# Output stage of a decoder layer: sixteen steps of two token tiles in place of eight steps of four

## The reference, cut to what matters

```python
z = out.reshape(B, H, S, dh).transpose(0, 2, 1, 3).reshape(B, S, L)   # (4, 1024, 256)
z = z @ Wo
z = _l2_normalize(z)
z = z @ Wff
z = _l2_normalize(z)
z = jax.nn.gelu(z, approximate=False)
...
x = _layernorm(x + z, axis=-1)      # mean, variance, (x - m) / sqrt(v + 1e-5)
```

## Time and profile before

| what | us |
|---|---|
| median of 3 runs | 1892.95 (1890.54 to 1895.87) |
| the profiled execution, its own time | 1888.5 |
| its span, first to last instruction | 1886.7 |
| first squares of the output stage, from the span's start | 1810.87 |
| mean granted TensorE clock, share of full speed | 0.988 |

### The profile page before, as it was taken

The page is one execution under the profiler, slowest core; times in us unless marked ns, Lnnn a source line. Parts: engine busy times, 40 slices in busy tenths (PEclk is TensorE's granted clock), DMA queues, the critical chain, the costliest instruction groups (busy, mean ns, idle before and its releaser), DMA issues. The chain is left out here.

```text
span 1886.7 us, 42906 instructions
## 1 busy us (share of the span) xinstructions
PE 1778.7 (94%) x16097; PEld 1195.6 (63%) x16198; DVE 1444.2 (77%) x2682; ACT 1518.7 (80%) x4462; POOL 669.8 (35%) x776
## 2 busy tenths in 40 slices
PE   6999999999999999899999989899999999999985
PEld 5888888888888888659999987622222222222232
DVE  6677777777777777456666655699999999999946
ACT  6777777777777777548898855699999999999964
POOL 2343344433333344405675630022222222222222
PEclk9999999999999999999999999999999999999998
DMA  7222323333333332431101006733453353345001
GB/s 179 46 63 63 63 63 60 61 64 63 57 64 63 61 65 54 106 102 41 45 16 44 18 21 163 203 46 46 62 73 46 46 82 54 46 65 71 1 23 67
DMA packets 139773, 121.61 MB, mean 64 GB/s; under 512 B 78876, under 2 KB 111536, under 8 KB 139568
## 3 DMA queue, kind: packets, MB, share of 16 engines
q1 hardware_dynamic: 139567, 118.88, 32.6%
HBM read 77.29 MB, written 41.53 MB: 63 GB/s over the span
## 5 line engine op out<-in xcount | busy, mean ns | idle before, releaser
L1961 DVE TENSOR_REDUCE s_neg_max<-s_ring 128x1 f32<-128x1024 f32 x512 | 580.7, 1295 | 7.0 <-PE s_ring L1879 6.8
L1921 ACT ACTIVATE s_prob<-s_ring,s_neg_max 128x1024 f32<-128x1024 f32 x512 | 569.8, 1114 | 4.1 <-DVE s_neg_max L1961 2.8
L1892 PE MATMUL s_acc<-s_prob,s_v_norm 128*32 128x256 f32 x4096 | 327.4, 393 | 1.9 <-POOL s_v_norm L1944 1.9
L1879 PE MATMUL s_ring<-f_stack 128*128 128x512 bf16 x923 | 288.5, 386 | 27.2 <-issue 17.6
L1940 POOL TENSOR_TENSOR s_row_inv<-s_row_sum,s_neg_one 128x4 f32<-128x4 f32 x128 | 128.8, 1007 | 410.7 <-ACT s_prob L1921 410.7
L1892 PEld LDWEIGHTS s_acc<-s_prob,s_v_norm 128*32 128x32 f32 x4096 | 81.7, 108 | 218.7 <-issue 215.4
L595 POOL TENSOR_SCALAR a_relu_ring<-a_qT 128x512 f32<-128x512 f32 x64 | 98.6, 1557 | 341.8 <-ACT a_qT L463 314.6
L1879 PEld LDWEIGHTS s_ring<-f_stack 128*128 128x128 bf16 x1024 | 58.5, 97 | 232.7 <-ACT s_prob L1921 221.8
L492 ACT ACTIVATE a_prob<-a_psum,a_neg_max 128x128 f32<-128x128 f32 x512 | 179.5, 400 | 21.4 <-DVE a_neg_max L703 21.4
L746 DVE SCALAR_TENSOR_TENSOR a_att<-a_psum,a_keep_cols,a_num_s 128x128 f32<-128x128 f32 x256 | 72.2, 345 | 133.1 <-ACT a_num_s L518 125.9
L1289 ACT ACTIVATE x_prob<-x_psum,x_neg_max 128x77 f32<-128x77 f32 x512 | 160.6, 337 | 14.1 <-DVE x_neg_max L1445 14.1
(11 more groups left out here) (196 smaller groups left out, 4036.8 us busy)
## 6 DMA issues: line engine op xcount, KB each, us to landing
f_stack<-qk_thirds SPq DMA_DIRECT2D x256, 128.0 KB, 7.4
segment_values<-a_v_stage SPq DMA_DIRECT2D x64, 256.0 KB, 3.2
a_v_pos<-segment_values SPq DMA_DIRECT2D x512, 32.0 KB
qk_thirds<-p_third SPq DMA_DIRECT2D x16, 768.0 KB, 7.7
a_x_in<-in_x_dram SPq DMA_DIRECT2D x16, 256.0 KB, 3.4
a_x_res<-in_x_dram SPq DMA_DIRECT2D x32, 128.0 KB, 2.9
after_attention<-a_normed SPq DMA_DIRECT2D x32, 128.0 KB, 2.4
x_x_in<-after_attention SPq DMA_DIRECT2D x32, 128.0 KB, 2.0
```

Of the source, the lines that this page charges most:

```text
L1879: last = pe.matmul(ring[n % 3][:, f * HALF:(f + 1) * HALF], k_stack[:, slot, j, kt * P:(kt + 1) * P], q_stack[:, slot, j, f * HALF:(f + 1) ...
L1892: last = pe.matmul(acc[32 * j:32 * j + 32, s], v_norm[:, step // KT % 2, step % 4, j, :], prob[:, step % 4, j, s], start=step % (2 * KT) = ...
L1921: act.activation(prob[:, step % 4, j, :], ring[n % 3][:, :], ACT.Exp, bias=neg_max[:, step % 2, j:j + 1], accum_out=row_sum[:, step % 4, j ...
L1961: dve.tensor_reduce(neg_max[:, step % 2, j:j + 1], ring[n % 3][:, :], AX_X, ALU.max, negate=True).then_inc(max_ready, 1)
```

## The change

Steps become two token tiles, sixteen of them. The matrix product and its PSUM are no longer counted in steps: PSUM is a ring of eight tiles (`SLOTS`), PE waits for tile t until the gelu of tile t-8 is done, and each gelu instruction raises the semaphore. In ACT's stream the look-ahead of squares is one tile instead of two. In DVE's stream the layer norm is split: `residual` keeps the addition and `g_stats`, and a new `variances` has `g_mean_var` and `g_var_eps`. `clamps(n+1)` and `factors(n+1)` now stand between the two. POOL runs `norms(n+1)` ahead of `deviations(n)`. The stores stay at two tiles each; their semaphores are counted by a helper `stores`. `COUNTS` is sixteen times 2, `FIRST[n]` is 2n, and `GT` stays 4 as the size of the small buffers.

```diff
-    STEPS = B * S // HALF
-    PER_BATCH = S // HALF
+    TILES = B * S // P
+    PER_BATCH = S // P
+    COUNTS = [GT // 2] * (2 * TILES // GT)
+    STEPS = len(COUNTS)
+    FIRST = [sum(COUNTS[:n]) for n in range(STEPS + 1)]
+    SLOTS = 8
...
+        def stores(n):
+            return 16 * sum(COUNTS[m] // 2 for m in range(n % 2, n + 1, 2))
...
         def _(pe):
-            for n in range(STEPS):
-                if n >= 2:
-                    pe.wait_ge(gelu_done, n - 1)
-                for t in range(GT):
-                    at = n % PER_BATCH * HALF + t * P
-                    for g in range(ZC):
...
+            for t in range(TILES):
+                if t >= SLOTS:
+                    pe.wait_ge(gelu_done, t - SLOTS + 1)
+                at = t % PER_BATCH * P
+                for g in range(ZC):
+                    last = pe.matmul(psum[:, t % SLOTS, :], zT_all[:, t // PER_BATCH, g, at:at + P], w_both[:, g, :],
+                                     start=g == 0, stop=g == ZC - 1)
+                last.then_inc(z_done, 1)
...
-                for t in range(GT):
-                    last = act.activation(z[:, n % 2, t * D:(t + 1) * D], psum[:, n % 2 * GT + t, D:2 * D], ACT.Gelu,
-                                          scale=both_inv[:, n % 2, t:t + 1])
-                last.then_inc(gelu_done, 1)
-
-            squares(0, range(0, 2))
+                for t in range(COUNTS[n]):
+                    act.activation(z[:, n % 2, t * D:(t + 1) * D], psum[:, (FIRST[n] + t) % SLOTS, D:2 * D], ACT.Gelu,
+                                   scale=both_inv[:, n % 2, t:t + 1]).then_inc(gelu_done, 1)
+
+            squares(0, range(0, 1))
             for n in range(STEPS):
-                squares(n, range(2, GT))
+                squares(n, range(1, COUNTS[n]))
                 if n + 1 < STEPS:
-                    squares(n + 1, range(0, 2))
+                    squares(n + 1, range(0, 1))
                 gelu(n)
...
+            norms(0)
             for n in range(STEPS):
-                norms(n)
+                if n + 1 < STEPS:
+                    norms(n + 1)
                 deviations(n)
...
             def residual(n):
-                dve.wait_ge(gelu_done, n + 1)
...
+                dve.wait_ge(gelu_done, FIRST[n] + c)
...
-                for t in range(GT):
+                for t in range(c):
                     last = dve.bn_stats(stats[:, t, :], y[:, n % 2, t * D:(t + 1) * D])
                 last.then_inc(ln_step, 1)
+
+            def variances(n):
+                c = COUNTS[n]
                 dve.wait_ge(ln_step, 2 * n + 1)
                 dve.memset(spare[:, :], 0.0)
-                for t in range(GT):
+                for t in range(c):
                     last = dve.bn_aggr(mean_var[:, n % 2, t, :], stats[:, t, :])
...
-            for n in range(STEPS):
-                clamps(n)
+            clamps(0)
+            factors(0)
+            for n in range(STEPS - 1):
+                residual(n)
+                clamps(n + 1)
                 if n >= 1:
                     normalise(n - 1)
-                factors(n)
-                residual(n)
+                factors(n + 1)
+                variances(n)
+            residual(STEPS - 1)
+            variances(STEPS - 1)
+            normalise(STEPS - 2)
             normalise(STEPS - 1)
```

More of the change, by code:

```diff
@@ L1979, in sem @@
             return ctx.enter_context(nc.semaphore("g_" + name))
-        psum = ctx.enter_context(nc.psum_tensor("g_psum", [P, 2 * GT, 2 * D], F32))
+        psum = ctx.enter_context(nc.psum_tensor("g_psum", [P, SLOTS, 2 * D], F32))
         neg_half = sb("neg_half", [P, 2 * GT])
@@ L2011, in _ @@
             for n in range(STEPS):
[L2012 to L2016, removed]
+                for pair in range(COUNTS[n] // 2):
+                    at = FIRST[n] + 2 * pair
+                    sp.wait_ge(o_ready, at // 2 + 1)
+                    sp.dma_start(outf[at * P:(at + 2) * P, :].rearrange("(t p) d -> p t d", p=P),
+                                 o_fin[:, n % 2, 2 * pair * D:(2 * pair + 2) * D].rearrange("p (t d) -> p t d", d=D)
                                  ).then_inc(stored[n % 2], 16)
-            for parity in range(2):
-                sp.wait_ge(stored[parity], 16 * STEPS)
+            for n in range(STEPS - 2, STEPS):
+                sp.wait_ge(stored[n % 2], stores(n))
         @block.tensor
         def _(pe):
-            for n in range(STEPS):
-                if n >= 2:
-                    pe.wait_ge(gelu_done, n - 1)
-                for t in range(GT):
-                    at = n % PER_BATCH * HALF + t * P
-                    for g in range(ZC):
-                        last = pe.matmul(psum[:, n % 2 * GT + t, :], zT_all[:, n // PER_BATCH, g, at:at + P],
-                                         w_both[:, g, :], start=g == 0, stop=g == ZC - 1)
-                    last.then_inc(z_done, 1)
+            for t in range(TILES):
[6 more added lines that the diff above has]
+                last.then_inc(z_done, 1)
         @block.scalar
@@ L2036, in squares @@
                 for t in tiles:
-                    act.wait_ge(z_done, n * GT + t + 1)
+                    act.wait_ge(z_done, FIRST[n] + t + 1)
                     for k in range(2):
-                        last = act.activation(unused[:, n % 2, k, t, :], psum[:, n % 2 * GT + t, k * D:(k + 1) * D], ACT.Square,
+                        last = act.activation(unused[:, n % 2, k, t, :],
+                                              psum[:, (FIRST[n] + t) % SLOTS, k * D:(k + 1) * D], ACT.Square,
                                               accum_out=sums[:, n % 2, k, t:t + 1])
-                if t == GT - 1:
-                    last.then_inc(squared, 1)
+                    if t == COUNTS[n] - 1:
+                        last.then_inc(squared, 1)
             def gelu(n):
@@ L2066, in norms @@
                 pool.wait_ge(clamps_ready, n + 1)
-                pool.tensor_tensor(roots[:, n % 2, :, :].rearrange("p a b -> p (a b)"),
-                                   clamped[:, n % 2, :, :].rearrange("p a b -> p (a b)"), neg_half[:, :], ALU.pow
+                c = COUNTS[n]
+                pool.tensor_tensor(roots[:, n % 2, :, 0:c], clamped[:, n % 2, :, 0:c],
+                                   neg_half[:, 0:2 * c].rearrange("p (a b) -> p a b", a=2), ALU.pow
                                    ).then_inc(roots_ready, 1)
@@ L2072, in deviations @@
                 pool.wait_ge(var_ready, n + 1)
-                pool.tensor_tensor(rstd[:, n % 2, :], var_eps[:, n % 2, :], neg_half[:, 0:GT], ALU.pow
+                c = COUNTS[n]
+                pool.tensor_tensor(rstd[:, n % 2, 0:c], var_eps[:, n % 2, 0:c], neg_half[:, 0:c], ALU.pow
                                    ).then_inc(rstd_ready, 1)
+            norms(0)
             for n in range(STEPS):
-                norms(n)
+                if n + 1 < STEPS:
+                    norms(n + 1)
                 deviations(n)
@@ L2082, in clamps @@
             def clamps(n):
-                at = 3 * n
+                at, c = 3 * n, slice(0, COUNTS[n])
                 dve.wait_ge(squared, n + 1)
-                dve.tensor_scalar(clamped[:, n % 2, 0, :], sums[:, n % 2, 0, :], 1e-24, None, ALU.max
+                dve.tensor_scalar(clamped[:, n % 2, 0, c], sums[:, n % 2, 0, c], 1e-24, None, ALU.max
                                   ).then_inc(norm_step, 1)
                 dve.wait_ge(norm_step, at + 1)
-                dve.reciprocal(first_inv[:, n % 2, :], clamped[:, n % 2, 0, :]).then_inc(norm_step, 1)
+                dve.reciprocal(first_inv[:, n % 2, c], clamped[:, n % 2, 0, c]).then_inc(norm_step, 1)
@@ L2089, in clamps @@
                 dve.wait_ge(norm_step, at + 2)
-                dve.tensor_tensor(scaled[:, n % 2, :], sums[:, n % 2, 1, :], first_inv[:, n % 2, :], ALU.mult
+                dve.tensor_tensor(scaled[:, n % 2, c], sums[:, n % 2, 1, c], first_inv[:, n % 2, c], ALU.mult
                                   ).then_inc(norm_step, 1)
                 dve.wait_ge(norm_step, at + 3)
-                dve.tensor_scalar(clamped[:, n % 2, 1, :], scaled[:, n % 2, :], 1e-24, None, ALU.max
+                dve.tensor_scalar(clamped[:, n % 2, 1, c], scaled[:, n % 2, c], 1e-24, None, ALU.max
@@ L2094, in clamps @@
                                   ).then_inc(clamps_ready, 1)
             def factors(n):
+                c = slice(0, COUNTS[n])
                 dve.wait_ge(roots_ready, n + 1)
-                dve.tensor_tensor(both_inv[:, n % 2, :], roots[:, n % 2, 0, :], roots[:, n % 2, 1, :], ALU.mult
+                dve.tensor_tensor(both_inv[:, n % 2, c], roots[:, n % 2, 0, c], roots[:, n % 2, 1, c], ALU.mult
                                   ).then_inc(both_ready, 1)
             def residual(n):
-                dve.wait_ge(gelu_done, n + 1)
@@ L2103, in residual @@
-                dve.tensor_tensor(y[:, n % 2, :], z[:, n % 2, :],
```

(11 more changed lines are left out.)

1 line of the change is left out of this document (added).

## The result

The changed kernel takes 1895.67 us (median of 22 runs, 1889.78 to 1900.18); the kernel before, over 22 runs of its own, 1891.80. The predicted 1895.7 was 2.8 us above the earlier median of 1892.95. That it falls on the measured median is partly luck, since the median of before moved by 1.15; the difference was forecast 1.6 too small. One of the 28 executions of before that were made beside experiments 1 to 4 took 2684.57 us at a mean granted clock of 0.594, and the ratios leave it out.

A forecast was written before the change was run, and what follows sets the result against it. The output stage was held to be bound by a loop through ACT, DVE and POOL, PE close below. Loop +10.9, start -5.1, end -3.0 gave +2.8 us on 1892.95, so 1895.7 us; range 1891.5 to 1900.0.

The forecast's parts named there:

- Start: Start of the output stage: gelu(0) comes 5.12 us earlier, at 1816.47, after tile 2's squares and the gelu table load.
- End: From the last gelu to the span's end: 7.45 us against 10.46, 3.0 less.
- Loop: Output stage's repeating steps: fifteen periods of 4.37 us, 65.55 against 54.67 before, so +10.9.
- Gelu to addition: From a step's gelu on ACT to the addition's start on DVE: 0.87 us for two tiles.
- addition to statistics: On DVE, from the 128x512 addition's start to `g_stats`: 0.73 us.
- statistics to the first clamp: On DVE, 0.67 us, the clamp not waiting for the statistics; upper bound 0.12 more if it waits.
- rival 1: Fixed parts of the loop at their upper bounds: period 4.56, +5.7 us in all, 1898.6; chance 0.13.
- Clamps to POOL: From the first of four clamps on DVE to POOL's start: 0.86 us, upper bound 0.07 more.
- Last distance: From `g_both_inv` on DVE to the next step's gelu on ACT: 0.20 us, as before.
- `g_roots` to `g_both_inv`: POOL's power on 128x4 taking 1.01 us, plus 0.03 to DVE's operation: 1.04 us.
- Rival 2: PE held 0.94 us a step, TensorE's clock falls to 1.2 GHz and PE paces: +5.7 us, 1898.7; chance 0.05.
- Rival 3: DVE and POOL overlap more, PE paces the stage at 1.72 us a tile: -12 us, 1880.9; chance 0.04.

The follow-up runs named there:

- experiment 1: The changed kernel with four-tile steps and the old orders of ACT, POOL and DVE, keeping only PSUM freed by token tile; ratio to before 1.0006.
- experiment 2: The changed kernel with four-tile steps in place of two, its order and ring kept; 1882.50 us, ratio to before 0.9946.
- experiment 3: The changed kernel's two-tile steps, ring and look-ahead, with POOL and DVE in the old order; 1900.94 us, ratio to before 1.0049.
- experiment 4: The changed kernel with normalise(n-1) moved behind factors(n+1) on DVE; 1894.98 us, ratio to before 1.0023.
- Experiment 5: The changed kernel with clamps(n+1) ahead of residual(n) on DVE and both squares of step n+1 ahead of gelu(n) on ACT; 1881.49 us, ratio to before 0.9945.
- experiment 7: The changed kernel with only clamps(n+1) ahead of residual(n) on DVE, squares unchanged; 1891.79 us in a single execution.
- experiment 6: The changed kernel's order and ring with steps of 2, seven times 4, and 2 tiles; 1885.16 us, ratio to before 0.9965.

## Why the prediction was right

**The sum.** Start -5.12 forecast, -5.15 measured in the profile (5.57 against 10.72). End -3.0 forecast, 7.44 - 10.46 = -3.02 measured. Loop +10.9 forecast; from gelu(0) to gelu(15) it is 66.44 us, against 54.65 from gelu(0) to gelu(7) before: +11.8. Together +3.6 against +2.8 forecast, and the timed runs say 4.4 (2.6 to 5.9). That the end came out to 0.03 is luck in part: the last `g_rstd` took 0.80 where I had 0.70, and from the last normalisation to the end of the span it was 2.95, not 3.07. The step of the argument that everything hung on, that `clamps(n+1)` behind `residual(n)` puts the clamps into the loop as `g_rstd` leaves it, is what the chain after shows.

**The terms of the loop.** Gelu to addition 0.87, addition to statistics 0.73, statistics to the first clamp 0.67 (1852.53 - 1851.86): all three as forecast; the clamp doesn't wait for the statistics, so the upper bound of 0.12 and with it half of rival 1 fall. Clamps to POOL 0.83, forecast 0.86. Last distance 0.19, forecast 0.20. Wrong was one term: `g_roots` to `g_both_inv` 1.15, forecast 1.04. Over the fourteen steps that have it this makes 1.5 us; the 0.04 a step by which the other terms came out shorter gives 0.6 back, and the loop was missed by 0.9.

**The step that failed.** I wrote that DVE's normalisation and POOL's power don't slow each other, from DVE's side: 1.38 beside the power and 1.39 without. I didn't ask it from POOL's side, and the output stage of before couldn't have shown it: there `g_roots` starts at 1858.75 to 1858.78, and the normalisation behind it, at 1858.82. In the change the order is turned round, and experiment 4 shows that this is the cause: with DVE idle the power is at 1.01 again. So the overlap was right for DVE and wrong for POOL, at 0.11 us a step.

The attention stage of the same trace of before did have such a delay, in operations of 512 columns, and I hadn't asked for it. Its timeline, POOL and DVE:

```profile
46.31 2.04 POOL L611 TENSOR_TENSOR a_prob<-a_prob,a_row_inv 128x512 f32<-128x512 f32 x2
...
87.31 2.48 POOL L611 TENSOR_TENSOR a_prob<-a_prob,a_row_inv 128x512 f32<-128x512 f32 x2
87.34 1.55 DVE L668 SCALAR_TENSOR_TENSOR a_e_ring<-a_e_ring,a_relu_ring 128x512 f32<-128x512 f32 x1
...
135.40 0.69 DVE L668 SCALAR_TENSOR_TENSOR a_e_ring<-a_e_ring,a_relu_ring 128x512 f32<-128x512 f32 x1
135.42 3.02 POOL L611 TENSOR_TENSOR a_prob<-a_prob,a_row_inv 128x512 f32<-128x512 f32 x2
```

Where DVE starts 0.02 ahead, the two products on POOL take 3.02 us in place of 2.04 (a second operation of the same kind starts on DVE at 136.61, beside the later product); where POOL starts 0.03 ahead, it is DVE's operation that takes 1.55 in place of 0.69.

**The rivals.** Rival 1, the upper bounds: the first clamp's fell, and POOL starts 0.25 behind the last clamp in the steady steps; only in the first is it 0.33. Rival 2, the clock: PE is stopped 0.74 in every 4.44 us after 22 tiles, as this rival had it (the loop's own paragraph said about 20), and the granted clock stays at 1.00. The forecast of 0.94 held in each step counted 3.43 us of products, and by that count it is 4.44 - 3.43 = 1.01; the 0.67 of before was read from the rows, where the last product's length is counted too, and is to be set against 0.74. The Trainium skill's account of PSUM banks in TensorE: Matmul & The Clock Gate, section on psum-queue depth-cycling, isn't seen at work here: with these stops the clock doesn't move. The fall of the clock ahead of this stage came behind the idle time of 1.95 us in the softmax stage. Rival 3, PE as pacer: not in the change, as argued. Experiment 5 shows that it is there to be had, 3.43 a step and 66.5 us for the stage, with two edits more.

**Where the gain went.** The change has two good parts and one that eats them. Its order, with the look-ahead of one tile, is worth 7 us and more (experiment 2); start and end get 8 us shorter, 1.7 of them by the look-ahead and the rest by the small steps. But a small step has a loop of 4.43 for two tiles, where the same order with four tiles takes 7.00: 0.93 us more for each two tiles.

**What stays open.** The timed runs of experiment 2 give 10 us (7 to 14), the profile of the stage 5.6, or 7 with the clock's scatter taken out; this is inside the interval, and I have nothing that separates the two. Why the clock comes back at different times was not looked into. What DVE and POOL share when a power begins is not shown; the runs show only which of them was running.

## What to carry to other kernels

Before cutting steps, write down the loop that sets the period and price it at the new size: each fixed part in it is paid per step, and halving the step doubles it. Small operations beside the loop cost nothing here (experiment 5), with no engine full, so the gain is in opening the loop, and that may need an edit in two streams at once, each of which alone shows nothing. When an operation is moved beside another, ask both engines' rows whether they slow each other, and look at which of the two starts first.

## What the hardware showed that I had not expected

- A power on POOL is slower when DVE has begun an addition or a normalisation just before it. 128x4: 1.01 us with DVE idle or with a normalisation that starts after it (experiment 3, 0.06 after), 1.11 behind a normalisation of two tiles that began 0.17 earlier, 1.38 and 1.44 behind an addition that began 0.18 and 0.12 earlier (experiments 7 and 5). 128x2: 0.69 alone, 0.80 behind a normalisation, 1.07 behind an addition. 128x8: 1.64 alone, 1.73 to 1.75 behind a normalisation of four tiles.
- The loss isn't one amount. Behind an addition it is 0.37 to 0.43, about 0.14 less than what was left of the addition as the power began. Behind a normalisation it is 0.10 where DVE is through before the power would end alone, and 0.24 where DVE goes on beyond that: 1.25 for 128x4 (experiments 2 and 6) and 0.93 for 128x2 (experiment 6).
- In the output stage the lengths of DVE's single instructions hardly changed: the addition is 0.68 to 0.69 and a normalisation of one tile 0.40 to 0.41 in all of them, also where an addition began while a power was running (0.69 at 1855.57 in the change, with `g_rstd` from 1855.12 to 1855.82). The 0.80 of the two normalisations at 1853.19 stands alone; in the other steps of the change they take 0.73 or 0.74. This doesn't hold in general: in the attention stage of before, an operation on DVE that began 0.03 behind one of 512 columns on POOL took 1.55 in place of 0.69.
- The clock of TensorE at the start of a stage differs between executions of one and the same code ahead of it. Where it was still at 1.2 GHz for the first 3.2 to 4.0 us, the first squares came 3.58 to 3.79 us behind PE's start, not 2.00.
